# Writing the high half of P with its own exponential, ahead of the exponential in place, in a gated cross-attention and expert kernel

## The chip, the cores and the metric

The kernel runs on one core of one Trainium2 chip. The metric is the device time of one execution in microseconds (us), as the median of several runs. The engines are named as in the profile: PE is TensorE's matmuls and PEld its weight loads, DVE is VectorE, ACT is ScalarE, POOL is GpSimd, SP is SyncE.

## The reference

A block with a gated cross-attention and a gated layer of eight experts. Sixteen sequences of 56 tokens look at 1500 context rows each, with 16 heads of 64; both sides are 128 wide.

```python
xn = _ln(x, ln1_s, ln1_b)
cn = _ln(context, lnc_s, lnc_b)
q = xn @ Wq
k, v = jnp.split(cn @ Wkv, 2, axis=-1)      # and one null key and value in front
sim = jnp.einsum('bhid,bhjd->bhij', q * scale, k)
attn = jax.nn.softmax(sim, axis=-1)
out = jnp.einsum('bhij,bhjd->bhid', attn, v)
out = _ln(out @ Wo, lno_s, lno_b)

x = x + jnp.tanh(g_xattn[0]) * attention(_layernorm(x), ctx_1024, ...)
x = x + jnp.tanh(g_ffn[0]) * experts(_layernorm(x), ...)
# experts: argmax of x @ wr + br picks one of 8; w1 (128x512), gelu, w2 (512x128)
```

## The kernel before, in words

Wq and Wk are folded into one 128x128 matrix per head, Wv and Wo into another, so that scores and values are products with the normalised context rows z themselves. For each of the 16 batches the 1500 context rows are cut into 12 chunks of 125 (index c), and all 16 heads times 56 queries stand side by side as 896 columns. Every matrix is held as a pair of fp16 halves, high and low, and a product is three matmuls: high by high, high by low, low by high.

One chunk goes like this. `sim` (line 1238) makes six matmuls into S: scores of 125 keys by 896 columns, in two banks of PSUM. S has four banks, so two chunks alternate in it (c % 2). `exps` (line 676) then runs an exponential on ACT in place, from S to S in fp32, with a bias column `mb` that carries a shift and the mask. `exps_hi` (line 681) copies the result on ACT to Ph, the fp16 high half of P, in SBUF. `sub` (line 967) on DVE subtracts Ph from the fp32 values in S and writes Pl, the low half. `pv` (line 1259) makes six matmuls of Ph and Pl by z into the accumulator A. P has room for four chunks (PB).

The order on each engine is written out in the program, with semaphores between engines. `sim_done` is counted by PE after a `sim`, `e_done` by ACT after an `exps`, `hi_done` by ACT after an `exps_hi`, `lo_done` by DVE after a `sub`, `pv_done` by PE after a `pv`. `ahead(b, c)` makes the scores, the exponential and the subtraction run two chunks ahead of the values: in slot c of batch b these steps treat chunk c + 2, and in slots 10 and 11 chunks 0 and 1 of the next batch. The wait of `sim` is on `lo_done` of the chunk two before, since that chunk's `sub` is the last reader of its banks of S.

In slots 0 to 6 PE also makes three matmuls per slot for the next batch's maxima (line 1298), which DVE reduces (line 1033): 21 per batch. Slots 7 to 11 have other work. ACT writes the shifts (line 752) after the pair of slot 7, half of a later batch's queries (line 700) after that of slot 9, and a row of null scores (line 707) after that of slot 10. In slot 11 ACT copies half of the accumulator (`a_copy`, line 766) between its exponential and its copy. PE makes the queries of a later batch in slot 8, and at the end of batches 2, 4 and so on to 14 also a projection of 48 matmuls (lines 1324 to 1326) in slot 11. Batch 15 has no next batch: PE then makes only `sim` and `pv`, and DVE does the normalisation of the first half of the tokens between its subtractions (lines 927 to 945), which PE transposes (line 1188) before the expert layer begins.

A boundary is named here by its batch: slots 7 to 11 of it and slot 0 of the next. Those of batches 2, 4, 6, 8, 10, 12 and 14 have the projection, those of batches 0, 1, 3, 5, 7, 9, 11 and 13 do not.

Of the kernel before, what the change touches and what calls it, by code (L numbers as in the profile page):

```python
# [5 lines left out]
def gated_cross_attention_moe_kernel(nc, x, ctx, mask, cols, rows, Wq, Wkv, Wo, wr, w1, b1, w2, b2,  # L6
# [21 lines left out]
    ACT = mybir.ActivationFunctionType  # L28
# [6 lines left out]
    DH = INNER // H  # L35
    NP = H // 2
    E, _, F = w1.shape
    FC = F // 128
    NC = 12
# [15 lines left out]
    PB = 4  # L55
# [13 lines left out]
    with es:  # L69
        def sb(name, shape, dt=fp32):  # L70
            return es.enter_context(nc.sbuf_tensor(name, shape, dt))

        def sem(name):
            return es.enter_context(nc.semaphore(name))
# [12 lines left out]
        Ph, Pl = PP[0:CK, 0], PP[0:CK, 1]  # L87
# [4 lines left out]
        mb = sb("mb", [CK, 2, NC])  # L92
# [129 lines left out]
        hi_done = sem("hi_done")  # L222
        e_done = sem("e_done")
# [72 lines left out]
        def ahead(b, c):  # L296

            return (b, c + 2) if c + 2 < NC else (b + 1, c + 2 - NC)
# [336 lines left out]
        def _(act):  # L635
# [13 lines left out]
            def xt_copy(i, scale, bias):  # L649

                act.wait_ge(xt_ready, i + 1)
                act.activation(xT[:, (i % 2) * GTOK:(i % 2 + 1) * GTOK], (A[:, i] if i < 2 else X[:, 1])[:, 0:GTOK],
                               ACT.Identity, scale=scale, bias=bias).then_inc(xt_copied, 1)
# [11 lines left out]
            def scores_of(c):  # L665
                return S[0:CK, 2 * (c % 2):2 * (c % 2) + 2, 0:HR]

            def exps(b, c, p):

                s = scores_of(c)  # L670
                act.wait_ge(sim_done, NC * b + c + 1)
                if not (isinstance(b, int) and NC * b + c < PB):
                    act.wait_ge(pv_done, NC * b + c + 1 - PB)
                if c == 0:
                    act.wait_ge(mb_done, b + 1)
                act.activation(s, s, ACT.Exp, bias=mb[:, p, c:c + 1]).then_inc(e_done, 1)  # L676

            def exps_hi(b, c):

                act.wait_ge(e_done, NC * b + c + 1)  # L680
                act.activation(Ph[:, c % PB, :].rearrange("p (a r) -> p a r", a=2), scores_of(c),  # L681
                               ACT.Copy).then_inc(hi_done, 1)

            def value_copy(k):

# [5 lines left out]
            def queries(n, p, j):  # L691

                query_hi(n, p, j, X[:, j, 0:HR])
                if j == 0:
                    act.wait_ge(null_in, 16 * n)
                null_scores(j, X[0:1, j, 0:HR])

            def query_hi(n, p, j, bank):
                act.wait_ge(q_ready, 2 * n + j + 1)
                act.activation(qh[:, p, j * HR:(j + 1) * HR], bank, ACT.Identity,  # L700
                               scale=rowmask[:, 0:1], bias=rowbias[:, 0:1]).then_inc(qhi_done, 1)

            def queries_null(n):

                act.wait_ge(null_in, 16 * n)
                act.wait_ge(qlo_done, 2 * n + 2)
                act.activation(nullrow[0:1, :].rearrange("o (a r) -> o a r", a=2), X[0:1, :, 0:HR], ACT.Identity,
                               scale=1.0 / W_SCALE, bias=rowbias[0:1, 0:1]).then_inc(null_done, 2)
# [5 lines left out]
            def body(b, p, f):  # L714
                nb, np_ = b + 1, 1 - p

                for c in range(NC):
                    exp_slot = (f["main"] and c + 2 < NC) or (f["prep"] and c + 2 >= NC)


                    if c == 11 and not f["main"]:
                        queries(b + 2, p, 1)
                    if exp_slot:
                        exps(*ahead(b, c), p if c + 2 < NC else np_)
                    if c == NC - 1 and f["main"] and f["prep"]:
                        a_copy(b, f["tail"])
                    if exp_slot:
                        exps_hi(*ahead(b, c))
                    if c == 7 and f["prep"]:
                        shifts(nb, np_)  # L730
                    if c == 9 and f["znext"] and f["main"]:
                        act.wait_ge(sim_done, NC * b + NC)
                        query_hi(b + 2, p, 0, X[:, 0, 0:HR])
                    if c == 10 and f["znext"] and f["main"]:
                        queries_null(b + 2)
                    if c == 10 and not f["main"]:

                        act.wait_ge(nv_ready, 1)
                        act.activation(NVb[:, :], A[0:TT, 0, 0:D], ACT.Copy).then_inc(m_copied, 1)
                        act.wait_ge(b1_ready, 1)  # L740
                        act.activation(b1T[:, :], A[:, 1, 0:E * FC], ACT.Copy).then_inc(b1_copied, 1)
                    if c == 10 and not f["main"]:
                        queries(b + 2, p, 0)
                    if c == 2 and f["main"]:
                        null_weight(b, p)
                    if f["group"] and c == 9:
                        xt_copy(2, 1.0, 0.0)

            def shifts(nb, np_):

                act.wait_ge(mt_ready, nb + 1)
                act.activation(qh[0:1, np_, :].rearrange("o (r t) -> o r t", t=RT),
                               X[0:1, :, :].rearrange("o a r -> o (a r)")[:, 0:R]
                               .rearrange("o (t r) -> o r t", t=RT), ACT.Copy).then_inc(slot_done, 1)

            def null_weight(b, p):

                act.wait_ge(t7_done, b + 1)
                act.activation(P07[:, p, :], t7[:, :], ACT.Exp, bias=shift0[:, 0:1]).then_inc(p0_done, 1)

            def a_copy(b, b_ge1):

                act.wait_ge(pv_done, NC * b + NC)
                if b_ge1:
                    act.wait_ge(an_done, b)
                act.activation(Af[:, 0:HR], A[:, 0, 0:HR], ACT.Copy).then_inc(a_copied, 1)
# [9 lines left out]
            act.wait_ge(ld_f, 16 * 4)  # L776
            act.activation(gates, gates, ACT.Tanh).then_inc(tanh_done, 1)
            body(-1, 1, flags(-1))
            for b in (0, 1):
                body(b, b % 2, flags(b))  # L780
            with act.Fori(2, B - 3, 2) as i:
                body(i, 0, STEADY[0])
                body(i + 1, 1, STEADY[1])
# [43 lines left out]
        def _(dve):  # L827
# [135 lines left out]
            def sub(b, c):  # L963

                k = c % PB
                dve.wait_ge(hi_done, NC * b + c + 1)
                dve.tensor_tensor(Pl[:, k, :].rearrange("p (a r) -> p a r", a=2),  # L967
                                  S[0:CK, 2 * (c % 2):2 * (c % 2) + 2, 0:HR],
                                  Ph[:, k, :].rearrange("p (a r) -> p a r", a=2), ALU.subtract).then_inc(lo_done, 1)
# [66 lines left out]
            def body(b, p, f):  # L1036
                nb, np_ = b + 1, 1 - p
                for c in range(NC):
# [22 lines left out]
                    if (f["main"] and c + 2 < NC) or (f["prep"] and c + 2 >= NC):  # L1061
                        sub(*ahead(b, c))
# [427 lines left out]
```

## Time and profile before

| what | value |
|---|---|
| median of 3 runs | 722.62 us (722.53 to 723.53) |
| profiled execution, its own time | 722.68 us |
| span of its trace | 720.9 us |
| PE, DVE, ACT, POOL busy | 95%, 82%, 68%, 54% |
| granted TensorE clock | 0.979 of full speed over the span, 1.00 in every stretch from 60 us on |

Times are from the start of the span. A matmul's end in the trace is modelled, and matmuls are pipelined, so that PE's starts say more than its ends. A row of the timeline has its start, how long it took, the engine, the line, the operation, output and input; in square brackets the idle time of that engine just before, and what ended it.

### The profile page before, as it was taken

Reading aid. Unit: us, or ns where it says so; the run is one execution under the profiler, and the core shown is the slowest. Engines: PE = TensorE matmul, PEld = TensorE weight load, DVE = VectorE, ACT = ScalarE, POOL = GpSimd, SP = SyncE. Lnnn points to the kernel's source line nnn. Section 1 sums busy time; section 2 is a strip of 40 time slices with the busy share of each in tenths; the row PEclk is TensorE's granted clock in tenths of the full one; section 3 lists DMA queues with packets and bytes.
Section 4 is the critical chain, followed back from the end, with each engine's and each line's share of the span. In section 5 each row is a group of like instructions: output and inputs, shape, how many; then the busy total and the mean of one; then the engine's idle time right before and its main releaser. Section 6 shows DMA issues by size and latency. Waiting matters only on the chain.

```text
span 720.9 us, 14913 instructions
## 1 busy us (share of the span) xinstructions
PE 681.9 (95%) x5041; PEld 404.0 (56%) x5041; DVE 589.1 (82%) x1030; ACT 493.8 (68%) x622; POOL 387.7 (54%) x462
## 2 busy tenths in 40 slices
PE   2698999999999999999999999999999999799997
PEld 2545555546555554565456545654565455387886
DVE  3975979787979798979897988888887866868776
ACT  1406677766776777676767677667767777778885
POOL 5668195866464746564656465646464153837100
PEclk9758999999999999999999999999999999999999
DMA  5824081447161616160606060606121201010000
GB/s 157 188 72 43 16 115 58 100 73 78 38 71 43 87 26 84 28 87 26 87 26 87 26 87 26 87 26 87 26 44 26 44 30 56 27 27 2 15 2 15
DMA packets 73993, 40.33 MB, mean 56 GB/s; under 512 B 61310, under 2 KB 68502, under 8 KB 73958
## 3 DMA queue, kind: packets, MB, share of 16 engines
q1 hardware_dynamic: 73525, 39.77, 33.0%
q8 instruction: 21, 0.34, 0.2%
q10 hardware_dynamic: 432, 0.10, 0.1%
q14 instruction: 15, 0.11, 0.1%
HBM read 26.65 MB, written 0.52 MB: 38 GB/s over the span
## 4 chain that ended last, share of the span: by engine, by line
PE 74%; DVE 8%; ACT 6%; POOL 4%; DMA 4%; issue 3%; SPq 0%; DVEq 0%; ACTq 0%; POOLq 0%
PE S L1238 24%; PE A L1259 23%; PE X L1298 10%; PE S L1395 4%; PE A L1412 3%; ACT S L676 2%; ACT PP L681 2%; DVE PP L967 2%; DMA zTh<-z_hi 2%; DMA raw<-ctx_dram 2%; PE X L1412 2%; PE A L1181 1%; PE X L1308 1%; PE X L1325 1%; PE X L1326 1%
## 5 line engine op out<-in xcount | busy, mean ns | idle before, releaser
L676 ACT ACTIVATE S<-S,mb 125x896 f32<-125x896 f32 x192 | 187.6, 977 | 156.1 <-PE S L1238 153.9
L967 DVE TENSOR_TENSOR PP<-S,PP 125x896 f16<-125x896 f32 x192 | 208.2, 1085 | 62.4 <-ACT PP L681 62.2
L1033 DVE TENSOR_REDUCE mx<-X 128x1 f32<-128x500 f32 x336 | 215.7, 671 | 18.0 <-PE X L1298 11.4
L1259 PE MATMUL A<-PP,z_hi 125*128 125x448 f16 x768 | 208.2, 352 | 0.0
L681 ACT ACTIVATE PP<-S 125x896 f16<-125x896 f32 x192 | 175.7, 915 | 5.6
L1298 PE MATMUL X<-zTh,qh 128*128 128x500 f16 x336 | 130.3, 394 | 10.0 <-DVE mx L1033 6.0
L1259 PE MATMUL A<-PP,z_lo 125*128 125x448 f16 x384 | 123.7, 352 | 0.0
L1259 PEld LDWEIGHTS A<-PP,z_hi 125*128 125x128 f16 x768 | 75.0, 98 | 69.9
L477 POOL TENSOR_TENSOR An<-Af,Rb 128x896 f32<-128x896 f32 x16 | 33.3, 2080 | 134.5 <-DMA Rb<-r_scratch 134.5
L1238 PE MATMUL S<-qh,zTh 128*128 128x448 f16 x384 | 104.1, 352 | 1.0 <-DVE PP L967 1.0
L1238 PE MATMUL S<-qh,zTl 128*128 128x448 f16 x384 | 104.0, 352 | 0.0
L1238 PE MATMUL S<-ql,zTh 128*128 128x448 f16 x384 | 103.9, 352 | 0.0
L1298 PEld LDWEIGHTS X<-zTh,qh 128*128 128x128 f16 x336 | 44.1, 132 | 48.7 <-DVE mx L1033 13.8
L1238 PEld LDWEIGHTS S<-qh,zTl 128*128 128x128 f16 x384 | 37.5, 98 | 35.1
L1238 PEld LDWEIGHTS S<-ql,zTh 128*128 128x128 f16 x384 | 37.2, 97 | 35.5
L1259 PEld LDWEIGHTS A<-PP,z_lo 125*128 125x128 f16 x384 | 37.1, 97 | 32.5
L473 POOL TENSOR_TENSOR z_lo<-zf,z_hi 125x508 f16<-125x508 f32 (+1 forms) x31 | 50.1, 1616 | 5.0 <-POOL z_hi L467 4.4
L1238 PEld LDWEIGHTS S<-qh,zTh 128*128 128x128 f16 x384 | 35.0, 97 | 31.6 <-DVE PP L967 8.8
L793 ACT ACTIVATE S<-S,b1T 128x448 f32<-128x448 f32 x64 | 38.9, 607 | 9.9 <-PE S L1395 8.0
L458 POOL TENSOR_TENSOR zf<-zf,rs 125x1536 f32<-125x1536 f32 x15 | 41.3, 2752 | 2.4 <-POOL zf L453 2.1
L453 POOL TENSOR_TENSOR zf<-raw,mu 125x1536 f32<-125x1536 f32 x15 | 41.3, 2752 | 0.2
L798 ACT ACTIVATE early<-S 128x448 f16<-128x448 f32 x64 | 34.8, 543 | 3.2
(205 smaller groups left out, 1136.3 us busy)
## 6 DMA issues: line engine op xcount, KB each, us to landing
raw<-ctx_dram SPq DMA_DIRECT2D x16, 750.0 KB
Rb<-r_scratch SPq DMA_DIRECT2D x16, 448.0 KB, 3.5
wst<-in_w_dram SPq DMA_DIRECT2D x16, 256.0 KB, 3.3
early<-in_Wkv_dram SPq DMA_DIRECT2D x2, 512.0 KB, 14.3
early<-in_Wq_dram SPq DMA_DIRECT2D x1, 512.0 KB, 5.4
Wo_s<-in_Wo_dram SPq DMA_DIRECT2D x1, 512.0 KB, 11.7
zTh<-z_hi SPq DMA_TRANSPOSE x32, 4.0
zTl<-z_lo SPq DMA_TRANSPOSE x32, 3.6
```

The source lines that it names most:

```text
L453: ins = pool.tensor_tensor(zf[:, :, :], raw[:, p], wide(mu[:, :]), ALU.subtract)
L458: ch.link(pool.tensor_tensor(zf[:, :, :], zf[:, :, :], wide(rs[:, :]), ALU.mult))
L473: pool.tensor_tensor(lo, z, hi, ALU.subtract).then_inc(done, 1)
L676: act.activation(s, s, ACT.Exp, bias=mb[:, p, c:c + 1]).then_inc(e_done, 1)
L681: act.activation(Ph[:, c % PB, :].rearrange("p (a r) -> p a r", a=2), scores_of(c), ACT.Copy).then_inc(hi_done, 1)
L793: act.activation(s, s, ACT.Gelu, scale=1.0 / W_SCALE, bias=b1T[:, FC * (n % E) + f:FC * (n % E) + f + 1]).then_inc(gf_done, 1)
L967: dve.tensor_tensor(Pl[:, k, :].rearrange("p (a r) -> p a r", a=2), S[0:CK, 2 * (c % 2):2 * (c % 2) + 2, 0:HR], Ph[:, k, :].rearrange("p ( ...
L1033: dve.reduce_max(mx4[:, np_].rearrange("q k t -> q (k t)")[:, j:j + 1], X[:, j % 2, 0:KB], AX).then_inc(mx_red, 1)
L1238: ins = mm(S[:, 2 * (c % 2) + a, 0:HR], z[:, p, c, :], q[:, p, a * HR:(a + 1) * HR], start=(n == 0), stop=(n == 2))
L1259: ins = mm(A[:, a, 0:HR], z[:, p, c, :], q[:, k, a * HR:(a + 1) * HR], start=(c == 0 and n < 2), stop=(c == NC - 1 and n >= 4))
L1298: mm(X[:, j % 2, 0:KB].rearrange("p (c k) -> p c k", k=CK), qh[:, np_, t:R:RT], zTh[:, np_, blk * KC:(blk + 1) * KC, 0:CK], start=True, st ...
L1412: ins = mm(YB[k % 3], gg[:, f, t * TT:(t + 1) * TT], w[:, e, 1, f * D:(f + 1) * D], start=(i == 0), stop=(i == 3 * FC - 1))
```

## The change

`exps` now reads the scores and writes the exponential to Ph in SBUF, with the bias column, and counts `hi_done`. Behind it `exps_full` waits for `hi_done` and runs the exponential in place, with the same bias column, and counts `e_done`. The copy is gone. `sub` waits for `e_done` in place of `hi_done`. `pv` still waits for `hi_done`. The second step of a pair stands where the copy stood, behind `a_copy` in slot 11.

```diff
@@ exps and what follows it @@
                 if c == 0:
                     act.wait_ge(mb_done, b + 1)
+                act.activation(Ph[:, c % PB, :].rearrange("p (a r) -> p a r", a=2), s, ACT.Exp,
+                               bias=mb[:, p, c:c + 1]).then_inc(hi_done, 1)
+
+            def exps_full(b, c, p):
+
+                s = scores_of(c)
+                act.wait_ge(hi_done, NC * b + c + 1)
                 act.activation(s, s, ACT.Exp, bias=mb[:, p, c:c + 1]).then_inc(e_done, 1)
-
-            def exps_hi(b, c):
-
-                act.wait_ge(e_done, NC * b + c + 1)
-                act.activation(Ph[:, c % PB, :].rearrange("p (a r) -> p a r", a=2), scores_of(c),
-                               ACT.Copy).then_inc(hi_done, 1)
@@ the body on ACT @@
                     if exp_slot:
-                        exps_hi(*ahead(b, c))
+                        exps_full(*ahead(b, c), p if c + 2 < NC else np_)
@@ sub on DVE @@
-                dve.wait_ge(hi_done, NC * b + c + 1)
+                dve.wait_ge(e_done, NC * b + c + 1)
```

The order on ACT, at a boundary, from the copy or exponential that ends slot 8 to the end of slot 11 (with the semaphores that each row waits for). Before:

```order
L681 ACTIVATE PP<-S 125x896 [waits e_done]
L676 ACTIVATE S<-S,mb 125x2x448 [waits pv_done,sim_done]
L681 ACTIVATE PP<-S 125x896 [waits e_done]
L700 ACTIVATE qh<-X,rowbias,rowmask 128x448 [waits q_ready,sim_done]
L676 ACTIVATE S<-S,mb 125x2x448 [waits mb_done,pv_done,sim_done]
L681 ACTIVATE PP<-S 125x896 [waits e_done]
L707 ACTIVATE nullrow<-X,rowbias 1x896 [waits qlo_done,null_in]
L676 ACTIVATE S<-S,mb 125x2x448 [waits pv_done,sim_done]
L766 ACTIVATE Af<-A 128x448 [waits an_done,pv_done]
L681 ACTIVATE PP<-S 125x896 [waits e_done]
```

The same place on ACT after the change, where PP is the tensor that holds Ph and Pl, and line numbers from 677 on are one higher:

```order
L683 ACTIVATE S<-S,mb 125x2x448 [waits hi_done]
L676 ACTIVATE PP<-S,mb 125x896 [waits pv_done,sim_done]
L683 ACTIVATE S<-S,mb 125x2x448 [waits hi_done]
L701 ACTIVATE qh<-X,rowbias,rowmask 128x448 [waits q_ready,sim_done]
L676 ACTIVATE PP<-S,mb 125x896 [waits mb_done,pv_done,sim_done]
L683 ACTIVATE S<-S,mb 125x2x448 [waits hi_done]
L708 ACTIVATE nullrow<-X,rowbias 1x896 [waits qlo_done,null_in]
L676 ACTIVATE PP<-S,mb 125x896 [waits pv_done,sim_done]
L767 ACTIVATE Af<-A 128x448 [waits an_done,pv_done]
L683 ACTIVATE S<-S,mb 125x2x448 [waits hi_done]
```

The number of instructions and their places are the same; in each pair the write to PP now stands first and the write to S second, and both read mb. On the other engines no instruction moved.

## Rows read from the trace of the kernel before

**Rows 1.** The page: busy time, share of the span and instructions of each engine.

```profile
PE 681.9 (95%) x5041; PEld 404.0 (56%) x5041; DVE 589.1 (82%) x1030; ACT 493.8 (68%) x622; POOL 387.7 (54%) x462
```

**Rows 2.** Waits: who waited for whom, us in total, times, longest.

```profile
DVE PP L967 <- ACT PP L681: 62.2, 69, 5.8
...
PEld S L1238 <- DVE PP L967: 8.8, 31, 1.2
```

**Rows 3.** ACT's lines one by one: duration ns min/median/max.

```profile
L676 ACT ACTIVATE S<-S,mb x192: 943/982/983, 60.2 to 619.1; 125x896 f32<-125x896 f32 x192
...
L681 ACT ACTIVATE PP<-S x192: 889/917/918, 61.2 to 620.2; 125x896 f16<-125x896 f32 x192
...
L752 ACT ACTIVATE qh<-X x16: 889/889/906, 55.1 to 585.2; 1x896 f16<-1x896 f32 x16
...
L707 ACT ACTIVATE nullrow<-X,rowbias x14: 982/982/982, 97.9 to 559.4; 1x896 f32<-1x896 f32 x14
```

**Rows 4.** ACT's groups by form: busy us, mean ns, idle before.

```profile
L798 ACT ACTIVATE early<-S 128x448 f16<-128x448 f32 x64 | 34.8, 543 | 3.2
...
L700 ACT ACTIVATE qh<-X,rowbias,rowmask 128x448 f16<-128x448 f32 x16 | 11.5, 719 | 0.0
```

**Rows 5.** Timeline of ACT, slots 9 to 11 of batch 5 (no projection).

```profile
271.62 0.98 ACT L676 ACTIVATE S<-S,mb 125x896 f32<-125x896 f32 x1 [1.58 <-PE S L1238]
272.64 0.92 ACT L681 ACTIVATE PP<-S 125x896 f16<-125x896 f32 x1
273.45 0.72 ACT L700 ACTIVATE qh<-X,rowbias,rowmask 128x448 f16<-128x448 f32 x1
274.06 0.98 ACT L676 ACTIVATE S<-S,mb 125x896 f32<-125x896 f32 x1
275.07 0.92 ACT L681 ACTIVATE PP<-S 125x896 f16<-125x896 f32 x1
275.88 0.98 ACT L707 ACTIVATE nullrow<-X,rowbias 1x896 f32<-1x896 f32 x1
276.77 0.94 ACT L676 ACTIVATE S<-S,mb 125x896 f32<-125x896 f32 x1
277.66 0.52 ACT L766 ACTIVATE Af<-A 128x448 f32<-128x448 f32 x1
278.09 0.89 ACT L681 ACTIVATE PP<-S 125x896 f16<-125x896 f32 x1
```

**Rows 6.** Timeline of DVE and PE, end of the same boundary.

```profile
279.01 1.09 DVE L967 TENSOR_TENSOR PP<-S,PP 125x896 f16<-125x896 f32 x1 [1.08 <-ACT PP L681]
...
280.74 0.42 PE L1298 MATMUL X<-zTh,qh 128*128 128x500 f16 x1 [0.39 <-DVE mx L1033]
```

**Rows 7.** Timeline of DVE, PEld and PE, boundary of batch 6 (with projection).

```profile
308.17 1.09 DVE L967 TENSOR_TENSOR PP<-S,PP 125x896 f16<-125x896 f32 x1 [0.50 <-ACT PP L681]
...
309.32 0.20 PEld L1238 LDWEIGHTS S<-qh,zTh 128*128 128x128 f16 x2 [0.18 <-DVE PP L967]
...
309.04 0.54 PE L1259 MATMUL A<-PP,z_hi 125*128 125x448 f16 x2
309.42 0.54 PE L1238 MATMUL S<-qh,zTh 128*128 128x448 f16 x2
...
315.92 2.25 DVE L1033 TENSOR_REDUCE mx<-X 128x1 f32<-128x500 f32 x3 [0.92 <-PE X L1298]
```

**Rows 8.** Timeline of ACT and DVE in slots with maxima (batch 6).

```profile
288.25 0.98 ACT L676 ACTIVATE S<-S,mb 125x896 f32<-125x896 f32 x1 [0.80 <-PE S L1238]
...
290.55 1.08 DVE L967 TENSOR_TENSOR PP<-S,PP 125x896 f16<-125x896 f32 x1
```

**Rows 9.** Timeline of DVE and PE, end of batch 15's scores.

```profile
616.56 1.09 DVE L967 TENSOR_TENSOR PP<-S,PP 125x896 f16<-125x896 f32 x1 [1.53 <-ACT PP L681]
617.57 2.34 DVE L944 TENSOR_TENSOR xn<-x_s,mu 112x512 f32<-112x512 f32 x1
...
621.31 0.60 PE L1188 MATMUL X<-idf,xn 112*128 112x112 f32 x4 [1.07 <-DVE xn L945]
```

## The prediction

> **What bounds the kernel now.** I read the busy shares first: PE works 95% of the span, ACT only 68%, so a change on ACT costs nothing by default and costs its whole price wherever PE waits for the chain through ACT [rows 1]. The second view is who waits for whom. DVE's `sub` waits for ACT's copy 69 times in 192, and PE's weight load of `sim` waits for a `sub` 31 times, 8.8 us in all [rows 2]. PE and PEld never wait for ACT's `PP` directly: the list of waits has no such row. The third view is the timeline at the places of these waits. There are four kinds.
>
> *Slots 0 to 6 of batches 0 to 14.* ACT waits 0.80 us for PE before its exponential, and the `sub` starts with no idle time in front, behind three reductions [rows 8]. Its operand was there at 288.25 + 0.98 + 0.03 + 0.92 = 290.18, and it began at 290.55, 0.37 us later. ACT has slack here.
>
> *Boundary without projection* (batches 0, 1, 3, 5, 7, 9, 11, 13; eight of them). From 271.62 to 278.98 ACT works without a hole: pair, query half, pair, null row, and the pair of slot 11 with the accumulator copy inside [rows 5]. The last copy releases `sub` at 279.01, then come the reductions, and PE stands still 0.39 us until the first one is done, at 280.74 [rows 6]. All this is one chain: three pairs in series, with PE at its end.
>
> *Boundary with projection* (batches 2, 4 to 12, six of them, and 14). `sub` ends at 308.17 + 1.09 = 309.26, the weight load starts at 309.32, takes 0.10, and the matmul starts at 309.42, which is 0.38 after the pair of matmuls at 309.04, the same step as within a `pv` [rows 7]. So PE loses nothing today, and there is nothing left either. One pair lies in this loop. The last pair does not count: the reductions behind it wait 0.92 us for PE, which has the projection to do.
>
> *Batch 15.* No maxima: a slot is 12 matmuls, two every 0.38 us [rows 7], so 2.28 us, and the loop `sim`, pair, `sub`, `sim` just fits into two slots, as above. Its last `sub` at 616.56 is followed by the normalisation, for which PE waits 1.07 us [rows 9].
>
> **The change part by part.** The number of ACT instructions stays. The copy without a bias column, from PSUM to SBUF in fp16, becomes an exponential with the column `mb` to the same place; the exponential in place stays as it is, behind the other. DVE's and PE's instructions stay. No DMA and no other queue is passed.
>
> *Price of the new instruction.* No row shows an exponential to SBUF. What the bias column costs is read from two rows of one partition by 896 columns: `L752`, a copy, takes 889 ns and `L707`, with a bias column, 982, so 93 ns [rows 3]. Both run behind an instruction for which they don't wait. The copy to Ph in the same situation, at the end of slot 11, also takes 889, and 917 where it waits for its partner [rows 3]. So the new exponential takes 917 + 93 = 1010 ns, or 982 without a wait, and the pair goes from 982 + 917 = 1899 to 1010 + 982 = 1992: 93 ns more. In slot 11 it goes from 943 + 889 to 982 + 943, again 93. Within a pair 0.03 us passes between the end of the first and the start of the second [rows 5]; the wait of the second for the first stays, under another name, so I leave that as it is.
>
> *Bounds of this price.* If the destination cost nothing, the new exponential would be equal to that in place, 982: 982 - 917 = 65 ns. From below: nothing if a bias costs nothing beside the table's work, and less than nothing if the second of the pair started before the first is done, as instructions without a wait do: `L707` starts at 275.88 while the copy before it ends at 275.99 [rows 5]. That saves 0.11 + 0.03 = 0.14, net 93 - 140 = -47 ns. From above: two pointer operands, as `L700` has them, cost 719 - 543 = 176 ns over a plain copy of the same shape [rows 4]. I take 93, since its two rows differ by this operand alone.
>
> The page ScalarE: Activation LUTs of the Trainium skill says under "Step-by-step: what each stage is for" that ScalarE's writes to PSUM are faster than those to SBUF. By that rule the exponential to SBUF is dearer than the one in place, which makes 93 ns and not 65 the price; without it the sum would be 2.3 us instead of 3.3. The rows lean to the rule: without a wait `L676` into PSUM takes 943 and `L707` into SBUF 982, both with one bias column and 896 columns [rows 3], though they differ in partitions too.
>
> *Earlier high half.* `hi_done` comes about 0.9 us earlier. It is worth nothing: `pv` of a chunk runs two slots behind its exponential, and no PE row waits for it. *`sub`* needs the second step of the pair as before, hence comes 93 ns later per pair on its chain.
>
> *Sum, in units of one pair's 93 ns on PE's path.* At the start (batch -1) the `sub` of chunks 0 and 1 of batch 0 hold PE up, two pairs in series: 2. Boundaries without projection: 8 x 3 = 24. With projection, batches 2 to 12: 6 x 1 = 6; batch 14: 1. Batch 15: the pair of chunk 2 delays `sim` of chunk 4, that of 4 delays 6; then DVE's own work for the tokens stands before the `sub`s and carries the delay on without adding; the pair of chunk 9 adds one more and hands it to the normalisation: 3. Together 36 units, 36 x 0.093 = 3.35 us. The other 156 of 192 pairs lie beside PE's work: in slots 0 to 6 under the 0.37 us above, which 0.093 does not use up. If that cover were gone, each of the 15 x 7 = 105 pairs would cost up to 0.093 more, 9.8 us. The expert layer starts later by the sum and is otherwise unchanged.
>
> The profiled execution took 722.68 us (span 720.9 and 1.8 around it), 0.06 above the median. 722.68 + 3.35 = 726.03; from the median it is 725.97. I predict 726.0.
>
> **The rivals.**
>
> *B, the destination is free:* 65 ns, 36 x 0.065 = 2.3 us, 725.0. For it: ACT's rows on one partition might not speak for 125. Against it: 982 against 943 above.
>
> *C, the boundaries absorb it:* in the boundaries without projection only the load of `sim` is held up, one unit, and the longer ACT chain ends in slack. Then 20 units, 1.9 us, 724.5. Against it: ACT has no hole from 271.62 to 278.98 and PE's wait at 280.74 is already there.
>
> *D, the new exponential costs what the copy did,* because the column is fetched beside other work or is cached from the pair: no change, 722.6. Against it: 982 against 889 in `L707` and `L752`, fourteen and sixteen times with hardly any spread.
>
> *E, faster:* the second exponential no longer needs the first one's result, only its turn. If it starts under the end of the first, the pair is 47 ns shorter, and the same 36 places give 1.7 us back: 721.0. It decides at one point: whether the second starts more than 0.06 us before the first ends (0.06 + 0.03 us of gap is the 93 ns). Against it: the program still waits for `hi_done`, which is counted when the first is complete.
>
> *F, dearer:* 176 ns, 6.3 us, 729.0, if reading bias and writing SBUF add up to more than the rows show.
>
> **How the numbers follow.** The forecast has 0.61, B 0.17, C 0.06, D 0.08, E 0.03, F 0.05. A measurement of this kernel can tell 0.2%, 1.45 us, from no change: 721.2 to 724.1. Forecast, B, C and F lie above, 0.89, of which I put 0.01 down for a smaller C: slower 0.88. D and that 0.01 are within: 0.09. E is faster: 0.03. The range goes from 724.1, below C, to 727.3, which is 36 x 0.13 = 4.7 us above before, a price between forecast and F; left out are D, E and most of F, 0.15.
>
> **What would show it.** The new exponential to PP at about 1010 ns against 915 for the copy, the one in place still at about 980 with 0.03 us between them; ACT busy up by 192 x 0.093 = 18 us, to about 512; PE's wait for the first reduction after a boundary without projection up by 0.28; such a boundary 0.28 us longer and one with projection 0.09; PE's busy time unchanged. I am wrong if the exponential to SBUF takes about 917 or under 960, if the second of a pair starts before the first has ended, or if slots 0 to 6 grow as well.

## The result, and the profile after

| | before | changed |
|---|---|---|
| median of 12 runs each | 722.77 us | 725.93 us |
| ratio | 1 | 1.0044, 95% interval 1.0034 to 1.0055 |
| span of the profiled execution | 720.9 us | 724.7 us |

The kernel became slower by 3.2 us, with an interval from 2.5 to 4.0. The forecast was 726.0.

The price first. The page of the changed kernel has the busy times, and the two lines of ACT, one by one, their durations (ns, min/median/max). They answer to [rows 1, 3]:

```profile
PE 685.4 (95%) x5041; PEld 403.8 (56%) x5041; DVE 587.5 (81%) x1030; ACT 513.0 (71%) x622; POOL 388.1 (54%) x462
```

```profile
L676 ACT ACTIVATE PP<-S,mb x192: 981/1007/1009, 60.5 to 622.9; 125x896 f16<-125x896 f32 x192
...
L683 ACT ACTIVATE S<-S,mb x192: 944/982/982, 61.5 to 624.0; 125x896 f32<-125x896 f32 x192
```

The exponential to SBUF takes 1007 ns where the copy took 917, and 981 where the copy took 889 without a wait. The one in place is what it was. ACT is busy 19 us longer, 192 times about 0.1. PE reads busy 3.5 us longer, where the forecast had it unchanged: 1.9 us of that lie before the first exponential, where nothing was changed, and the rest is waiting that the modelled ends of its rows cover.

Then the waits of the changed kernel (us in total, times, longest), which answer to [rows 2]:

```profile
DVE PP L968 <- ACT S L683: 70.5, 69, 5.9
...
PEld S L1239 <- DVE PP L968: 12.2, 31, 1.3
...
PE X L1299 <- DVE mx L1034: 6.8, 9, 1.1
```

Again 69 subtractions wait, and 31 weight loads, a little longer in sum. One new place appears in the list, the weight load of the projection; it is shown below.

The timeline of ACT at the boundary of batch 5, without projection, is the counterpart of [rows 5]:

```profile
273.45 1.01 ACT L676 ACTIVATE PP<-S,mb 125x896 f16<-125x896 f32 x1 [1.49 <-PE S L1239]
274.49 0.98 ACT L683 ACTIVATE S<-S,mb 125x896 f32<-125x896 f32 x1
275.39 0.72 ACT L701 ACTIVATE qh<-X,rowbias,rowmask 128x448 f16<-128x448 f32 x1
276.00 1.01 ACT L676 ACTIVATE PP<-S,mb 125x896 f16<-125x896 f32 x1
277.04 0.98 ACT L683 ACTIVATE S<-S,mb 125x896 f32<-125x896 f32 x1
277.95 0.98 ACT L708 ACTIVATE nullrow<-X,rowbias 1x896 f32<-1x896 f32 x1
278.84 0.98 ACT L676 ACTIVATE PP<-S,mb 125x896 f16<-125x896 f32 x1
279.73 0.52 ACT L767 ACTIVATE Af<-A 128x448 f32<-128x448 f32 x1
280.15 0.94 ACT L683 ACTIVATE S<-S,mb 125x896 f32<-125x896 f32 x1
```

And DVE and PE at its end, which answer to [rows 6], with two rows of the kernel before and then those of the changed one:

```profile
274.83 0.54 PE L1238 MATMUL S<-qh,zTh 128*128 128x448 f16 x2
...
277.17 0.55 PE L1238 MATMUL S<-qh,zTh 128*128 128x448 f16 x2
```

```profile
276.66 0.54 PE L1239 MATMUL S<-qh,zTh 128*128 128x448 f16 x2
...
279.21 0.55 PE L1239 MATMUL S<-qh,zTh 128*128 128x448 f16 x2
...
281.13 1.09 DVE L968 TENSOR_TENSOR PP<-S,PP 125x896 f16<-125x896 f32 x1 [1.38 <-ACT S L683]
...
282.87 0.42 PE L1299 MATMUL X<-zTh,qh 128*128 128x500 f16 x1 [0.78 <-DVE mx L1034]
```

From the first exponential to the end of the last, ACT works 280.15 + 0.94 - 273.45 = 7.64 us in one piece, against 278.98 - 271.62 = 7.36 before. DVE waits 1.38 us for it instead of 1.08. PE pays in two places. The `sim` of slot 0 starts at 279.21, 2.04 us later than its counterpart at 277.17, where the `sim` before it had been 1.83 later: 0.21 from the first two pairs, through the subtraction of chunk 0. The first reduction lets PE go at 282.87, 2.13 later than before: another 0.09 from the third pair. PE's idle time there reads 0.78 against 0.39 because at this batch the kernel before had lost 0.3 us a little earlier; at five of the other seven such boundaries it reads 0.69 or 0.70 before, so that the usual growth of this wait is 0.09. The boundary is 0.3 us longer.

To see where the whole delay arises I compared the starts of the 192 subtractions in both traces, at like places. The delay grows by 0.29 to 0.31 at each of the eight boundaries without projection, by 0.09 to 0.11 at each of the six with one before batch 14, by 0.08 at that of batch 14, by 0.23 in the first two chunks, and by nothing in slots 0 to 6. In batch 15 the last subtraction is no later than at the end of batch 14 (more on that below). The trace has two more steps that are not the change's. One of 0.30 is there before the first exponential. One of 0.21 is in batch 2, where PE waits for the transposed rows of z, 1.71 us here and 1.50 before. In the traces of the runs below this wait reads anything from 0.85 to 2.76 us, whatever was done to the pairs. The sum is 0.23 + 8 x 0.295 + 6 x 0.10 + 0.08 = 3.3 us, and with the two foreign steps 3.8, the difference of the spans.

The boundaries with a projection show something that I had not forecast. Three views of the changed kernel there, PEld and PE at batch 6, and who waits in front of the projection's first line:

```profile
311.54 0.11 PEld L1239 LDWEIGHTS S<-qh,zTh 128*128 128x128 f16 x2 [0.27 <-DVE PP L968]
...
313.88 0.13 PEld L1325 LDWEIGHTS X<-Mh,Anh 128*112 128x112 f16 x1 [0.33 <-ACT nullrow L708]
```

```profile
311.17 0.54 PE L1260 MATMUL A<-PP,z_hi 125*128 125x448 f16 x2
311.55 0.55 PE L1239 MATMUL S<-qh,zTh 128*128 128x448 f16 x2
```

```profile
L1325 PE MATMUL X<-Mh,Anh x128: 219/219/263, 171.3 to 652.0; 128*112 128x128 f16 x128
its engine sat idle before it (us, times) until:
  ACT nullrow L708: 2.0, 6
```

The weight load of `sim` comes 0.09 us later than in the step of before [rows 7], but the matmul is still 0.38 behind its forerunner: the load starts at 311.54 and the matmul at 311.55. PE loses nothing there. It loses its 0.10 two microseconds later, since the projection writes into X and has to wait until ACT has read the null row from it, behind two dearer pairs. In the kernel before, no line of that view names the null row. These are PE's first two matmuls of the projection, before and changed:

```profile
311.69 0.22 PE L1324 MATMUL X<-Mh,Anh 128*112 128x128 f16 x1
311.75 0.22 PE L1325 MATMUL X<-Ml,Anh 128*112 128x128 f16 x1
```

```profile
313.88 0.26 PE L1325 MATMUL X<-Mh,Anh 128*112 128x128 f16 x1
313.98 0.22 PE L1326 MATMUL X<-Ml,Anh 128*112 128x128 f16 x1
```

The first comes 0.44 us instead of 0.38 behind the pair of matmuls before it (313.44, and 311.31 before), and the second 0.10 instead of 0.06 behind the first: 0.06 and 0.04.

### The profile page after: what moved, and what is told of

Read it like the earlier page. It is cut to its first block, busy times and chain, and to the rows that moved or that the text cites. A ratio compares the mean times of both kernels' runs of the same rounds, so it can differ in the third digit from the quotient of the medians.

```text
span 724.7 us, 14913 instructions
## 1 busy us (share of the span) xinstructions
PE 685.4 (95%) x5041; PEld 403.8 (56%) x5041; DVE 587.5 (81%) x1030; ACT 513.0 (71%) x622; POOL 388.1 (54%) x462
## 4 chain that ended last, share of the span: by engine, by line
PE 75%; DVE 6%; ACT 6%; DMA 4%; POOL 4%; issue 3%; SPq 1%; DVEq 0%; ACTq 0%; POOLq 0%
PE S L1239 24%; PE A L1260 23%; PE X L1299 10%; PE S L1396 4%; PE A L1413 3%; ACT PP L676 2%; ACT S L683 2%; DMA early<-in_Wkv_dram 2%; DMA zTh<-z_hi 2%; PE X L1413 2%; DVE PP L968 2%; PE X L1325 1%; PE A L1182 1%; PE X L1309 1%; PE X L1176 1%
## 5 line engine op out<-in xcount | busy, mean ns | idle before, releaser
L676 ACT ACTIVATE PP<-S,mb 125x896 f16<-125x896 f32 x192 | 192.8, 1004 | 140.4 <-PE S L1239 140.0
L1239 PEld LDWEIGHTS S<-qh,zTh 128*128 128x128 f16 x384 | 33.5, 97 | 35.0 <-DVE PP L968 12.2
```

The lines of the kernel that those rows point to most:

```text
L1239: ins = mm(S[:, 2 * (c % 2) + a, 0:HR], z[:, p, c, :], q[:, p, a * HR:(a + 1) * HR], start=(n == 0), stop=(n == 2))
```

## The experiments

Each group of runs has its own fresh runs of the kernel before, and each ratio is to these: their median is 722.67 us for the two runs of an Identity or a copy in all places and the two of its split that read no column, 722.37 for the four with a column or two, and 722.39 for the last four. The ratios differ a little from the quotients of the medians.

**The price by itself.** Two runs keep the order of before and put another step in the place of the copy. The first:

```diff
-                               ACT.Copy).then_inc(hi_done, 1)
+                               ACT.Identity).then_inc(hi_done, 1)
```

> The order of before, in-place exponential first, but the step behind it is an Identity, which reads a bias column of zeros, where it was a plain copy. Theory (the price is the bias column alone): this step takes 1007 ns as the new exponential does, against 915, and the kernel is as slow as the changed one, 3.2 us over before, about 725.9. Rival 1 (the exponential itself, or writing the high half first, costs): the step costs less than 960 ns or the kernel stays within 1 us of before. Rival 2 (the earlier high half gives some time back in the changed kernel): this one is slower than the changed one, by over 1 us.

Measured: 722.55 us, ratio 1.0004 (0.9989 to 1.0018). The theory was not tested, because its premise failed: in ACT's group by form (busy us, mean ns, idle before) the Identity reads no second operand.

```profile
L681 ACT ACTIVATE PP<-S 125x896 f16<-125x896 f32 x192 | 175.7, 915 | 5.6
```

An Identity without a given bias costs what a copy costs. Two more runs (below) had the same flaw. The second run gives the column:

```diff
+        zeros = sb("zeros", [128, 1])          # set to 0.0 at the start
-                               ACT.Copy).then_inc(hi_done, 1)
+                               ACT.Identity, bias=zeros[0:CK, 0:1]).then_inc(hi_done, 1)
```

> The run with the Identity showed that it reads no column unless one is given. Now the order of before with an Identity that is given a bias column of zeros in place of the copy. Theory (the price is the bias column alone): the step takes 1007 ns against 915, and the kernel is 3.2 us over before, about 725.9. Rival 1 (the exponential itself is what costs 92 ns): 915 to 960 ns and within 1 us of before. Rival 2 (the earlier high half gives time back in the changed kernel): over 1 us slower than the changed one.

Measured: 725.54 us, ratio 1.0040 (1.0029 to 1.0051). The same view of this run:

```profile
L683 ACT ACTIVATE PP<-S,zeros 125x896 f16<-125x896 f32 x192 | 193.0, 1005 | 5.7
```

An exponential is not needed for the loss, nor another order: the column alone makes the step 90 ns dearer and the kernel as slow as the changed one, within the intervals. Rivals 1 and 2 fall. At boundaries without projection the delay grows by 0.28 here, against 0.30 in the changed kernel, with projection mostly by 0.04 against 0.10. By these steps of the traces the column alone makes 2.7 of the 3.3 us, and the order together with it the other 0.5; the medians cannot tell the two kernels apart. Where the 0.5 comes from is explained under what had not been expected.

**The order by itself.** The changed kernel with a plain copy in front:

```diff
-                act.activation(Ph[...], s, ACT.Exp,
-                               bias=mb[:, p, c:c + 1]).then_inc(hi_done, 1)
+                act.activation(Ph[...], s,
+                               ACT.Copy).then_inc(hi_done, 1)
```

> The order of the changed kernel, high half first and the exponential in place behind it, but the first step is a plain copy of the scores without a bias column (this leaves the exponential out of the high half). Theory: the copy takes 915 ns, the pair costs what it did before, and the kernel is within 0.7 us of before, 722.8. Rival 1 (order or early high half matter for themselves): 1 us or more away from before, below it if the early high half helps PE, above it if the subtraction that waits for a write to PSUM is released later.

Measured: 723.08 us, ratio 1.0006 (0.9997 to 1.0015). The group of this run:

```profile
L676 ACT ACTIVATE PP<-S 125x896 f16<-125x896 f32 x192 | 175.4, 914 | 153.7 <-PE S L1239 151.8
```

An earlier high half gains nothing, and a subtraction released by a write to PSUM instead of one to SBUF loses next to nothing: 0.01 to 0.05 us at each boundary without projection, 0.17 in all.

**Where it costs.** The dearer step only in one set of slots, the plain copy in the others (of the two new lines each run has one, and the comments are not in the code):

```diff
-                        exps_hi(*ahead(b, c))
+                        exps_hi(*ahead(b, c), (f["prep"] and c < 7 and f["main"]) or not f["prep"])   # cover
+                        exps_hi(*ahead(b, c), f["prep"] and (c >= 7 or not f["main"]))                # boundary
```

First with the Identity that reads no column, so that nothing was dearer; 722.38 (0.9984 to 1.0002) and 722.57 us (0.9988 to 1.0006) say only that this changes nothing:

> The dearer step (Identity with a bias column for the copy) only in slots 0 to 6 of batches 0 to 14 and in the ten slots of batch 15: 115 of the 192 pairs. Theory (these are covered: in slots 0 to 6 the subtraction starts 0.37 us after its operand is there, and in batch 15 the trace of the changed kernel gains no delay): within 0.7 us of before, 722.8. The sum on record has 0.28 us for batch 15: 723.1. Rival (every dear pair costs alike): 115/192 of 3.2 us, 1.9 us, 724.7.

> The dearer step only in slots 7 to 11 of batches 0 to 14 and at the start: 77 of the 192 pairs. Theory: all of the cost, 3.2 us, about 725.9, with steps of 0.28 to 0.30 us at the eight boundaries without projection and of 0.09 at the six with one. Rival (every dear pair costs alike): 77/192 of 3.2 us, 1.3 us, 724.1.

Then with the column:

> The Identity with a bias column of zeros for the copy only in slots 0 to 6 of batches 0 to 14 and in the ten slots of batch 15: 115 of the 192 pairs. Theory: covered, within 0.7 us of before, 722.7. The sum on record has 0.28 us for batch 15: 723.0. Rival (every dear pair costs alike): 115/192 of 3.2 us, 1.9 us, 724.6.

> The same dearer step only in slots 7 to 11 of batches 0 to 14 and at the start: 77 of the 192 pairs. Theory: all of the cost, 3.2 us, about 725.9, in steps of 0.28 to 0.30 us at the eight boundaries without projection and of 0.09 at the six with one. Rival (every dear pair costs alike): 1.3 us, 724.0.

| dearer step in | pairs | median | ratio |
|---|---|---|---|
| slots 0 to 6 and batch 15 | 115 | 722.69 us | 1.0006 (0.9994 to 1.0019) |
| slots 7 to 11 and the start | 77 | 724.75 us | 1.0032 (1.0019 to 1.0044) |

The 115 pairs cost nothing that the median can tell (its interval reaches from 0.4 us faster to 1.4 slower), and in their trace the delay grows by at most 0.01 us at every boundary before batch 14. Batch 15 is another matter. Its ten dear pairs put the subtractions of slots 6 and 7 0.10 us behind those of the kernel before, counted from slot 3 of batch 14. The trace of the kernel before is an odd yardstick there: in the traces of all five kernels whose pairs cost what its own do (the three with an Identity that reads no column, the copy first, and DVE's copy below) these subtractions come 0.07 to 0.08 us earlier than in it. Against those five the ten pairs cost 0.18 there, two pairs' price. How much of it reaches the end cannot be told, since at the last subtraction the five lie between 0.10 before and 0.18 after the kernel before.

The 77 have steps of 0.28 to 0.29 at each of the eight boundaries without projection and 0.04 to 0.05 at the six with one, as in the run with the column in all 192. The median's 2.4 us is less than the 3.2 expected, whose interval reaches 3.2; the steps that the edit makes in its trace add up to 0.19 + 8 x 0.285 + 6 x 0.045 + 0.08 = 2.8. By pairs alone it would have been 1.3, just outside the interval's lower end of 1.4; it is the steps in the traces that decide against that rival.

The whole span of that trace says little, as its profiled execution took 728.29 us. In batch 2 PE waited 2.76 us for the transposed rows of z, and behind this wait the granted clock was 0.50 from 154 to 157 us, the lower of its two levels (1.2 GHz), where matmuls of 448 columns start every 0.37 us instead of 0.19. Against the trace of before the two cost 2.9 us. The same is in the traces of two runs below, twice the price (a wait of 2.15 us) and all together (1.92 us), but not in that without the wait inside a pair (2.08 us). So the steps are read place by place, and not as a difference of spans.

**Twice the price.** The changed kernel with a second column:

```diff
-                act.activation(Ph[...], s, ACT.Exp,
+                act.activation(Ph[...], s, ACT.Exp, scale=ones[0:CK, 0:1],
                                bias=mb[:, p, c:c + 1]).then_inc(hi_done, 1)
```

> The changed kernel with a second column, a scale of ones, on the exponential that writes the high half. Theory: 1007 + 90 = about 1100 ns, 185 over the copy. Start 0.4, eight boundaries without projection 8 x 3 x 0.185 = 4.4, six with one 6 x (2 x 0.185 - 0.09 of slack before the projection) = 1.7, batches 14 and 15 about 0.5 since the loop over S now exceeds its slack of 0.09: together 7 us over before, 729.8. Rival (the sum on record, without slack anywhere): 36 x 0.185 = 6.7 us, 729.4; the trace tells them apart at the boundaries with projection, 0.28 against 0.19. Rival (slack takes part of any further delay): under 728.

Measured: 729.83 us as the median of 6 runs, ratio 1.0094 (1.0073 to 1.0115), which is 5.3 to 8.3 us and can't tell 7 from 6.7. Its ACT line:

```profile
L678 ACT ACTIVATE PP<-S,mb,ones x192: 1074/1097/1099, 59.6 to 628.1; 125x896 f16<-125x896 f32 x192
```

The second column costs another 90 ns. The delay grows by 0.56 to 0.57 at a boundary without projection (twice 0.28) and by 0.30 to 0.31 with one, where the sum on record wanted 0.19. These are PE's rows at batch 6:

```profile
314.10 0.54 PE L1262 MATMUL A<-PP,z_hi 125*128 125x448 f16 x2
314.56 0.55 PE L1241 MATMUL S<-qh,zTh 128*128 128x448 f16 x2
```

The `sim` is now 0.46 behind its forerunner and no longer 0.38, 0.09 late; another 0.18 follows at the projection. In batch 15 three `sim`s lose 0.09 each in the same way. That is the mark of a slack of 0.09: with a price of 0.09 it hides it, with 0.18 the half is seen.

**The wait inside a pair.** In the changed kernel both exponentials read the scores; the second needs no result of the first.

```diff
             def exps_full(b, c, p):
                 s = scores_of(c)
-                act.wait_ge(hi_done, NC * b + c + 1)
                 act.activation(s, s, ACT.Exp, bias=mb[:, p, c:c + 1]).then_inc(e_done, 1)
```

> The changed kernel in which the exponential in place doesn't wait for the high half: both only read the scores, and the second overwrites them behind the first on the same engine. Theory: the second starts 0.11 us before the first ends, as instructions without a wait do, and takes 943 ns: a pair of 1.84 us against 1.93 before and 2.02 in the changed kernel, from the first's start to the second's end. At a boundary without projection two of three pairs gain 0.09 on before and the third, with the accumulator copy inside, loses 0.09: 8 x 0.09 = 0.7 us, 722.0. Rival (the engine serialises two accesses to the same banks anyway): no overlap, 725.9.

Measured: 722.70 us, ratio 1.0004 (0.9992 to 1.0016) to before; one of its 12 runs took 1016 us, with a granted clock of 0.66 over the run where the others had 0.975 to 0.981. It hardly moves the median, and what lowered the clock is not known. Its timeline at the boundary of batch 5:

```profile
271.88 1.01 ACT L676 ACTIVATE PP<-S,mb 125x896 f16<-125x896 f32 x1 [1.64 <-PE S L1238]
272.79 0.97 ACT L682 ACTIVATE S<-S,mb 125x896 f32<-125x896 f32 x1
273.68 0.73 ACT L700 ACTIVATE qh<-X,rowbias,rowmask 128x448 f16<-128x448 f32 x1
```

The second starts 0.10 before the first ends, so the engine does overlap them, but it takes 0.97 and not 0.94: the pair is 1.88 us, against 1.94 in [rows 5] and 2.02 in the changed kernel. At a boundary the two shorter pairs pay for the third, with the accumulator copy inside, and the chain is as long as before (7.35 us). So the whole loss comes back (the interval is 0.6 us faster to 1.2 slower than before, and the boundaries before batch 14 are within 0.02 us of those in the trace of before), but not the 0.7 us beyond it.

**The chain that holds PE.** In the kernel before, all of the accumulator copied by DVE, with no copy on ACT in slot 11 (and the waits on the second semaphore dropped):

```diff
-                    if c == NC - 1 and f["main"] and f["prep"]:
-                        a_copy(b, f["tail"])                   # on ACT
@@ on DVE @@
-                        a_half(b, f["tail"])
+                        a_copy(b, f["tail"])
```

> Before, with the accumulator copied in slot 11 wholly by DVE (one copy of 896 columns in place of half on each engine). Theory (at a boundary without projection ACT's chain to the last subtraction holds PE): ACT's third pair ends 0.43 us earlier, and PE's wait of 0.39 to 0.70 us for the first reduction shrinks by about 0.4: 8 x 0.4 = 3.3 us less, 719.4. Rival (DVE is the bound there): DVE's longer copy, 1.1 us against 0.62, gives it back, within 0.7 us of before.

Measured: 720.86 us, ratio 0.9985 (0.9971 to 1.0000), so 1.5 us less by the medians, with an interval from 2.1 to nothing, and not the 3.3 of the theory. The trace says more. ACT and DVE at the end of batch 5's boundary:

```profile
275.55 0.94 ACT L675 ACTIVATE S<-S,mb 125x896 f32<-125x896 f32 x1
276.53 0.92 ACT L680 ACTIVATE PP<-S 125x896 f16<-125x896 f32 x1
```

```profile
276.08 1.09 DVE L1008 COPY Af<-A 128x896 f32<-128x896 f32 x1 [0.19 <-PE A L1255]
277.48 1.09 DVE L964 TENSOR_TENSOR PP<-S,PP 125x896 f16<-125x896 f32 x1 [0.30 <-ACT PP L680]
```

The last pair takes 1.90 us instead of 2.21 [rows 5], and each of the eight boundaries is 0.30 shorter, 2.4 us in all, those with a projection not at all. That is the chain of the forecast, seen from the other side. It is 0.3 and not 0.43 because the accumulator copy had stood in the gap in which the pair's second step waits for its first: without it the gap of 0.04 and the longer form of the copy come back.

The same edit in the changed kernel:

> The changed kernel with the accumulator copied wholly by DVE. Theory: as in the other run ACT's chain is 0.43 us shorter, but the three pairs still stand in series, so that the change costs about what it costs without this edit: 3 us over the run before this one, 722.6. Rival (the room that the edit makes swallows the 0.28 us of a boundary): under 1 us over the run before this one.

Measured: 724.00 us, ratio 1.0030 (1.0019 to 1.0041), which is 3.1 us over the run before this one, as the theory had it. The room that the edit makes does not swallow the price: the pairs still stand in series.

**All together.** The changed kernel without the wait, with DVE's copy, and with the null row's bias as an immediate:

```diff
-                act.activation(nullrow[...], X[0:1, :, 0:HR], ACT.Identity,
-                               scale=1.0 / W_SCALE, bias=rowbias[0:1, 0:1]).then_inc(null_done, 2)
+                act.activation(nullrow[...], X[0:1, :, 0:HR], ACT.Copy,
+                               scale=1.0 / W_SCALE, bias=-1.0).then_inc(null_done, 2)
```

> The changed kernel with three edits: no wait of the exponential in place for the high half, the accumulator copied wholly by DVE, and the null row with its bias as an immediate instead of a column (0.89 for 0.98 us). Theory: ACT's work from the chunk-11 scores of a boundary to its last pair is 0.27 + 0.43 + 0.09 = 0.8 us shorter than before, PE's waits for the first reduction (0.4 to 0.7 us, eight times) go away: 4.5 to 5.5 us under before, 717.5 to 718.5. Rival (DVE's own work is next in line there): no faster than the run with DVE's copy alone, 719.4.

Measured: 718.82 us, ratio 0.9957 (0.9940 to 0.9974): 3.6 us faster than before by the medians, with an interval from 1.9 to 4.3, and the fastest of all kernels run. Neither expectation holds: it is short of the 4.5 of the theory, and 2.0 us faster than the run with DVE's copy alone. The end of batch 5's boundary on DVE, and PE's wait:

```profile
277.62 1.09 DVE L1008 COPY Af<-A 128x896 f32<-128x896 f32 x1 [0.27 <-PE A L1255]
278.80 1.09 DVE L964 TENSOR_TENSOR PP<-S,PP 125x896 f16<-125x896 f32 x1
```

```profile
280.54 0.42 PE L1294 MATMUL X<-zTh,qh 128*128 128x500 f16 x1 [0.24 <-DVE mx L1030]
```

ACT's chain is 6.83 us, 0.53 shorter than before, and seven of the eight boundaries are 0.51 to 0.53 shorter. At that of batch 9 only 0.05 is left, since there PE waits 0.74 us for the transposed rows of z, and in batch 15 the trace loses 0.4. DVE's subtraction now starts without a wait for ACT, right behind its own longer copy, so the rival is right about what comes next: the last 0.24 us at this place are DVE's. What the immediate in the null row is worth by itself was not run.

## Why the prediction was right, and where it was not

*The price.* Forecast 93 ns, measured 90 (1007 - 917, and 1005 - 915 with the column alone). Deriving it from two rows of one partition held for 125. That the destination counts was right too: with one bias column 1007 to SBUF and 982 to PSUM, and without a wait 981 and 944. The output type is not the reason, as far as the null row may be compared, which goes to SBUF in fp32 and takes 982. The Trainium skill, page ScalarE: Activation LUTs, "Step-by-step: what each stage is for", says the same of the two ports; the rows here show 25 ns, and 37 without a wait.

*Boundaries without projection.* Forecast 8 x 3 x 0.093 = 2.23 us, measured 8 x 0.295 = 2.36. The chain is as described; where PE would show it was not: I had all of the 0.28 at the wait for the reduction, which grew by 0.09, and two of the three pairs arrive earlier, at the `sim` of slot 0. Moving the accumulator copy showed it from the other side.

*Boundaries with projection.* The step that failed is the sentence that in the loop over S "there is nothing left". The weight load starts as soon as the subtraction is done and the matmul may start 0.01 us behind the load (311.54 and 311.55); that the load took 0.10 is no time in which the matmul has to wait. So the loop had 0.09 us of slack, just the price of one column. The 0.56 us came all the same, 0.60 measured, from a wait that the prediction does not have: the projection behind the null row, two pairs late, less its own slack. The null row stands there only as a part of the chain at the other boundaries. Twice the price gave 0.30 and showed both. So the 0.56 was right in size by luck.

*Batch 15.* Forecast 3 units, 0.28 us. Against the trace of before nothing is left of them at the last subtraction, but that trace is an odd yardstick there: against the five others two of the three arrive at slots 6 and 7. The second, that of chunk 4, is the one that the slack in the loop over S hides. How much reaches the end is open. *The start* had 0.23 for 0.19, batch 14 0.08 for 0.09.

*Cover.* Slots 0 to 6 cost nothing, in the changed kernel and with the column there alone. None of the signs of being wrong came: the new exponential took 1007 ns, no second step started before its first had ended, and slots 0 to 6 did not grow.

The total of 3.35 us against 3.3 in the trace is closer than its terms: 0.28 of batch 15 that this trace does not show stands against 0.2 that boundaries and start had more. That 726.0 is only 0.1 us from the measured median is luck to that extent, and the median's own interval is 1.5 us wide. Of the rivals, B to F all fall. E, the second exponential starting under the first, is real once the wait is taken away, and worth the 3.2 us or so of the whole loss; in the changed kernel the wait kept it from happening.

## What to carry to other kernels

An operand can be what an instruction costs: a per-partition bias or scale column on a ScalarE instruction was 90 ns each, for an Exp as for an Identity, so compare the operand lists of two variants before their functions. Price such a change only where its engine has no hole between PE's last product and the wait of PE; the 105 dearer instructions in slots 0 to 6 were free here, and eight places made 2.4 of the 3.3 us. And where a rewrite turns a true dependency into two reads of the same input, take the wait away with it: that alone brought back all that the rewrite had cost.

## What had not been expected of the hardware

- PE's matmul started 0.01 us after the start of its weight load, where that load was late (311.54 and 311.55). The 0.10 us of the load's row are no part of the path there, in front of matmuls of 448 columns. Where a late load stood in front of matmuls of 128 columns, at the projection, the first of them started with the load too (313.88), but the second came 0.10 instead of 0.06 us behind it.
- An instruction that does not wait starts 0.11 us before the end of a copy to SBUF (275.88 and 275.99 in [rows 5]) but only 0.08 before the end of an exponential in place (275.39 and 275.47). So the null row starts 277.95 - 273.45 = 4.50 us after the chain's first exponential in the changed kernel, against 4.26 before [rows 5], 0.24 later behind two pairs that are dearer by 0.18. With the column on a last step that writes to SBUF it comes 4.44 us after it, 0.18 later, and with the order changed but a plain copy in front 4.32, 0.06 later. About 0.14 of these is slack in front of the projection, which is why the boundaries with a projection grow by 0.10 in the first, by 0.04 in the second and by nothing in the third.
- Two ScalarE instructions that read the same banks of PSUM, the second overwriting them, overlapped by 0.10 us without a wait. The second took 0.97 us, between the 0.94 of the one behind the accumulator copy and the 0.98 with a wait.
- An Identity without a bias of its own costs what a copy costs, 915 ns.
